# Token numbers laid on 125 partitions by three broadcast loads instead of spread by TensorE

## The reference

```python
w_emb = fake_quant(emb_weight)                 # [125, 128], scale = max|w| / 127
e = w_emb[y]                                   # [8, 512, 128]
x = pad(e, one position in front)
h = relu(depthwise conv of x with 2 taps)      # taps fake-quantized too
h = h + scan(layernorm(h))                     # linear recurrence, 4 heads of 64, normed and mixed
h = h + experts(layernorm(h))                  # 8 experts, 128 -> 512 -> 128, gelu
```

## Time and profile before

| | |
|---|---|
| median of 3 runs | 173.47 us (173.04 to 173.54) |
| the profiled execution | 173.62 us |
| its span, first to last instruction | 171.8 us |
| TensorE busy | 161.1 us, 94% |
| VectorE busy | 131.8 us, 77% |
| ScalarE, Pool busy | 100.1 us, 106.9 us |
| read from memory | 5.15 MB |

### The profile page before, as it was taken

The page is one execution under the profiler, slowest core; times in us unless marked ns, Lnnn a source line. Parts: engine busy times, 40 slices in busy tenths (PEclk is TensorE's granted clock), DMA queues, the critical chain, the costliest instruction groups (busy, mean ns, idle before and its releaser), DMA issues.

```text
span 171.8 us, 3460 instructions
## 1 busy us (share of the span) xinstructions
PE 161.1 (94%) x1149; PEld 137.7 (80%) x1149; DVE 131.8 (77%) x401; ACT 100.1 (58%) x232; POOL 106.9 (62%) x174
## 2 busy tenths in 40 slices
PE   5977999998999999999999999999999999998892
PEld 2666775895765799887668999999999999988791
DVE  3979959735448385997995998989889895668983
ACT  3038999442223532324326867859778597787691
POOL 4437678579995133460403794988969789698600
PEclk9999999999999999999999999999999999999999
DMA  4996000000000000000000000010100101001103
GB/s 147 370 427 257 4 0 2 0 6 0 0 0 0 4 0 0 0 6 0 0 0 0 0 4 0 4 63 0 56 11 0 63 0 65 0 0 67 59 2 122
DMA packets 2181, 7.46 MB, mean 43 GB/s; under 512 B 238, under 2 KB 748, under 8 KB 1908
## 3 DMA queue, kind: packets, MB, share of 16 engines
q1 hardware_dynamic: 2146, 7.23, 10.9%
q10 hardware_dynamic: 18, 0.02, 0.1%
HBM read 5.15 MB, written 2.10 MB: 42 GB/s over the span
## 4 chain that ended last, share of the span: by engine, by line
PE 67%; POOL 13%; issue 7%; ACT 5%; DVE 4%; DMA 2%; POOLq 1%; ACTq 0%; DVEq 0%
PE bank L1305 8%; PE bank L1285 8%; PE bank L1234 7%; PE bank L1149 6%; POOL hid_p L538 6%; PE bank L1143 5%; PE bank L1080 4%; PE bank L1030 4%; PE bank L1086 4%; PE bank L1231 3%; PE bank L1254 3%; POOL rstd L521 3%; PE bank L1111 2%; POOL res L549 2%; PE bank L1055 2%
## 5 line engine op out<-in xcount | busy, mean ns | idle before, releaser
L538 POOL TENSOR_TENSOR hid_p<-hid_f,hid_p 128x256 fp32r<-128x256 f32 x52 | 37.2, 739 | 15.4 <-ACT hid_p L686 13.8
L684 ACT ACTIVATE hid_f<-bank,pa 128x256 f32<-128x256 f32 x64 | 30.7, 487 | 17.5 <-PE bank L1285 14.7
L1285 PE MATMUL bank<-xaT_p,fc_p 128*128 128x256 f32 x192 | 34.8, 293 | 0.2 <-issue 0.2
L1305 PE MATMUL bank<-hid_p,out_hi 128*128 128x256 f32 x128 | 33.0, 293 | 1.7 <-POOL hid_p L538 1.1
L1285 PEld LDWEIGHTS bank<-xaT_p,fc_p 128*128 128x128 f32 x192 | 26.7, 190 | 0.3 <-issue 0.3
L1305 PEld LDWEIGHTS bank<-hid_p,out_hi 128*128 128x128 f32 x128 | 23.3, 188 | 3.6 <-POOL hid_p L538 2.3
L686 ACT ACTIVATE hid_p<-bank,pa 128x256 fp32r<-128x256 f32 x48 | 23.4, 487 | 0.0
L1234 PE MATMUL bank<-pb,xh 128*128 128x128 f32 x128 | 19.5, 275 | 0.0
L521 POOL TENSOR_TENSOR rstd<-spread,neg_half 128x8 f32<-128x8 f32 x8 | 13.2, 1646 | 9.5 <-DVE spread L933 9.5
L1305 PE MATMUL bank<-hid_p,out_lo 128*128 128x256 f32 x64 | 17.8, 279 | 0.0
L1234 PEld LDWEIGHTS bank<-pb,xh 128*128 128x128 f32 x128 | 16.9, 192 | 0.0
(11 more groups left out here) (156 smaller groups left out, 375.0 us busy)
## 6 DMA issues: line engine op xcount, KB each, us to landing
fc_w<-in_fc SPq DMA_DIRECT2D x2, 2048.0 KB, 11.5
out<-res SPq DMA_DIRECT2D x7, 256.0 KB, 2.0
pa<-in_pack_a SPq DMA_DIRECT2D x1, 407.0 KB, 3.2
pb<-in_pack_b SPq DMA_DIRECT2D x1, 384.0 KB, 4.2
out<-res SPq DMA_DIRECT2D x2, 128.0 KB, 1.7
pw<-in_pack_a SPq DMA_DIRECT2D x1, 64.0 KB, 3.2
emb_w<-in_emb SPq DMA_DIRECT2D x1, 62.5 KB
conv_w<-in_conv ACTq DMA_DIRECT2D x1, 1.0 KB
```

What stands on the lines that cost most here:

```text
L538: nc.gpsimd.tensor_tensor(hid_p[1][:, half, c, :], hid_f[:, m % HID_SLOTS, :], hid_p[0][:, half, c, :].bitcast(F32), ALU.subtract).then_in ...
L684: full = nc.scalar.activation(hid_f[:, m % HID_SLOTS, :], src, ACT.Gelu, bias=bias)
L1285: last = mm(fc1_bank(8 * b + n)[:, 0:HALF], fc1_p[w][:, e * HID + c * P:e * HID + (c + 1) * P], xaT_p[m][:, b % 2, half, :], start=(k == 0 ...
L1305: last = mm(out_bank(b, half)[:, half * HALF:(half + 1) * HALF], out_p[w][:, e, c * CH:(c + 1) * CH], hid_p[m][:, half, c, :], start=(c == ...
```

## The change

The integers go straight to 125 partitions. Three loads on ACT's queue read the token numbers of batch 0, of batches 1 to 3 and of batches 4 to 7, each with the partition as its outermost dimension of size 125 and a source that is the same for every partition. `ids_all` takes 16 KB on each of 125 partitions, in the place that `out_hi` takes over later. `one_hot` reads the integers from SBUF and waits for a load at batches 0, 1 and 4. `ids_i`, `ids_b`, `ident_b`, Pool's two casts and one memset, and `spread_ids` with its semaphore are gone; two more products of zeros stand where TensorE spread the first four batches. A tile `spare` keeps the other tiles where they were.

```diff
--- before.py
+++ after.py
+        with ExitStack() as until_gathered:
+
+            ids_all = until_gathered.enter_context(nc.sbuf_tensor("ids_all", [VOC, NB, L], I32))
...
-            ids_i = sb_early("ids_i", [NB, L], I32)
-            ids_b = sb_early("ids_b", [P, L], BF16)
-            ident_b = sb_early("ident_b", [P, P], BF16)
+            spare = sb_early("spare", [P, 832])
...
-        ld_ids, ld_emb, ld_pa, ld_pb = sem("ld_ids"), sem("ld_emb"), sem("ld_pa"), sem("ld_pb")
+        ld_ids = [sem("ld_ids0"), sem("ld_ids1"), sem("ld_ids2")]
+        ld_emb, ld_pa, ld_pb = sem("ld_emb"), sem("ld_pa"), sem("ld_pb")
...
-        def ids_bank(b):
-            return bank[{2: 3, 3: 6}.get(b, b % 2)][0:VOC, :]
...
+        IDS_PARTS = ((0, 1), (1, 4), (4, NB))
...
-                nc.gpsimd.memset(ids_b[:], 0.0).then_inc(pool_const, 1)
-                pool.wait_ge(ident_ready, 2)
-                nc.gpsimd.tensor_copy(ident_b[:], ident).then_inc(ids_ready, 1)
...
-                pool.wait_ge(pool_const, 6)
-                pool.wait_ge(ld_ids, 16)
-                nc.gpsimd.tensor_copy(ids_b[0:NB, :], ids_i[:]).then_inc(ids_ready, 1)
...
                 act.dma_start(conv_w[:], conv).then_inc(ld_conv, 16)
-                act.dma_start(ids_i[:], ids).then_inc(ld_ids, 16)
+                for n, (b0, b1) in enumerate(IDS_PARTS):
+                    act.dma_start(ids_all[:, b0:b1, :], ids[b0:b1].unsqueeze(0).broadcast_to([VOC, b1 - b0, L])
+                                  ).then_inc(ld_ids[n], 16)
...
                 def one_hot(b):
-                    dve.wait_ge(idb_done, b + 1)
+                    for n, (b0, _) in enumerate(IDS_PARTS):
+                        if b == b0:
+                            dve.wait_ge(ld_ids[n], 16)
                     if b >= OH_SLOTS:
                         dve.wait_ge(gat_done, b - OH_SLOTS + 1)
-                    nc.vector.tensor_scalar(onehot[:, b % OH_SLOTS, NCH:EXT * NCH], ids_bank(b), float(VOC - 1),
+                    nc.vector.tensor_scalar(onehot[:, b % OH_SLOTS, NCH:EXT * NCH], ids_all[:, b, :], float(VOC - 1),
                                             number[0:VOC, :], ALU.min, ALU.is_equal).then_inc(oh_ready, 1)
 
-                dve.wait_ge(pool_const, 6)
+                dve.wait_ge(pool_const, 5)
...
-                def spread_ids(b):
-                    if b > 3:
-                        pe.wait_ge(oh_ready, (1, 2, 5, 6)[b - 4])
-                    mm(ids_bank(b), ident_b[:, b:b + 1].broadcast_to([P, VOC]), ids_b[:], start=True,
-                       stop=True).then_inc(idb_done, 1)
-
...
-                pe.wait_ge(pool_const, 6)
+                pe.wait_ge(pool_const, 5)
...
-                pe.wait_ge(ids_ready, 2)
-                spread_ids(0)
-                spread_ids(1)
-                spread_ids(2)
-                pe.wait_ge(amax_all_ready, 1)
-                spread_ids(3)
-                keep_clock(1)
+                keep_clock(3)
...
-                    if 3 < b + 3 < NB:
-                        spread_ids(b + 3)
```

More of the change, by code:

```diff
@@ L207, in build @@
         pool_link, dve_link = sem("pool_link"), sem("dve_link")
-        ids_ready, amax_e_ready, tab_ready = sem("ids_ready"), sem("amax_e_ready"), sem("tab_ready")
+        amax_e_ready, tab_ready = sem("amax_e_ready"), sem("tab_ready")
         attn_g_ready, taps_ready = sem("attn_g_ready"), sem("taps_ready")
         amax_t_done, taps_done = sem("amax_t_done"), sem("taps_done")
-        idb_done, oh_ready, gat_done, h_ready = sem("idb_done"), sem("oh_ready"), sem("gat_done"), sem("h_ready")
+        oh_ready, gat_done, h_ready = sem("oh_ready"), sem("gat_done"), sem("h_ready")
         st1_ready, mv1_ready, rstd1_ready, u_ready = (
```

## The result

The changed kernel takes 199.88 us (median of 4 runs, 199.42 to 200.00) against 173.34 us for the kernel before, run alongside. The ratio is 1.152, 95% interval 1.150 to 1.155. The forecast was 194.0. Its mechanism was given 189 to 199, the whole range was 186 to 200. So the direction is right and the size 6 us short; the measured time lies 0.9 us above the mechanism's own range and 0.1 us inside the wider one.

What follows compares the result with a forecast made beforehand. TensorE, busy 94% of 171.8 us, bounds the kernel, so head delays reach the end in full. 173.6 + 20.1 - 0.5 - 0.5 + 1.5 = 194.2, or 194.0 us against the runs' median; mechanism 189 to 199, range 186 to 200.

Steps and rivals of the forecast that it cites:

- Five engines: New loads at the head: 125 rows are carried by five engines, 25 rows each, 410 KB on each.
- Which load is last, and what it holds up: Head: the third load lands last and delays the fifth one-hot; the second, at 18 to 22 us, costs nothing beyond.
- When it lands: Third load's landing: 31.3 us (30.1 to 33) at 26.6 GB/s per engine; fifth one-hot moves from 11.19, +20.1 us.
- Given back in the rounds: Behind the wait, up to batch 7: two savings of 0.5 us each.
- The first term: Behind the fifth one-hot: statistics of batch 2 follow after about 3.0 us instead of 3.46, -0.5 us.
- The second was nothing: Rounds up to batch 7: shorter one-hots and missing products save 0.5 us (0 to 2.9).
- The slow pace of TensorE: After TensorE's idle time: slower gathers, transposes and powers, 1.2 us a round for none to three rounds, +1.5 us.
- The shorter one-hot: VectorE's one-hot reading SBUF instead of PSUM: 0.45 us taken, bounds 0.29 to 0.75, against 0.75 before.
- The sixteen-engine case: Rival, chance 0.06: the new loads spread over all 16 engines, third landing between 12.6 and 20.3 us; 173.5 to 182.
- Slow reads of a shared stretch: Rival, chance 0.04: reading one stretch of memory 125 times runs at two thirds of the rate; about 202 or more.
- The prologue's 0.4 us: Prologue ahead of the rounds: its own gain of some 0.4 us, expected to drown in the wait.
- ScalarE's queue first: Rival, chance 0.07: the five engines serve ScalarE's queue first, 410 KB land at 17.8 us; about 179.5 to 181.

Runs made afterwards that it cites:

- the run with TensorE busy through the wait: The changed kernel with 20 more products of zeros ahead of the first transposes, where TensorE waited for the third load; 198.82 us.
- The half version: The kernel before, with only batches 4 to 7 laid by one 128-row load behind pack_b, TensorE spreading the first four; 173.95 us, ratio 1.002.
- the run with own stretches: The changed kernel with each of the 125 rows reading its own stretch of the fc1 weights instead of the shared token numbers; 198.93 us.

## Why the prediction was right, and where it was short

The path was right: five engines, the third load, and the wait in front of the fifth one-hot. The landing time was not, and that the measured 199.88 still lies within the stated range is luck: the range went to 200 for the tails of the rivals, while my own sum ended at 199.

**Five engines: right.** The small packets of before told it, 15 more of them appeared, and every run with another row count followed.

**Which load is last, and what it holds up: right.** The third load, then VectorE's fifth one-hot, and behind it TensorE's transposes. The second load came at 27.5, not at 18 to 22, and stayed without cost of its own.

**When it lands: the term that was too small.** Predicted 31.3, measured 37.3, which is the whole error: +20.1 should have been +26.1. The bytes were right. From 20 us on 2.14 MB were still moved, nearly all by the five engines (in the first of these microseconds the others were still ending). These have 3.70 MB in all, so they had done some 1.6 MB by then, 320 KB each in the 17.7 us from 2.3 on: an estimated 18 GB/s. At the 26.6 that I took from the earlier trace rows it would have been 12.0 us; the missing 5.7 us are nearly all of the error. I took the rate of engines whose rows are all dealt alike; beside rows dealt otherwise all 16 together ran at 241 to 283 GB/s over 3 to 15 us. My upper end of 33 was no bound for this: it left contention out.

**Given back in the rounds: 0.5 + 0.5 predicted, 0.7 measured**, from the run with TensorE busy through the wait. The first term, the statistics of batch 2 that need not wait, was 1.0: they come 2.5 us behind the one-hot (37.30 to 39.78), not 3.46. The second was nothing: 0.3 was lost again, by the difference, for which no run gives a cause. The half version shows some 0.2 won in steady rounds.

**The slow pace of TensorE: 1.5 predicted, 1.1 measured.** It was over by the gather at 44.69.

**The shorter one-hot: 0.45 taken, 0.48 measured**, against 0.75 from PSUM.

**The rivals.** ScalarE's queue was not served first. The sixteen-engine case was put at 173 to 182; made real by 128 rows it is 177.6, and in line of need 173.75. Slow reads of a shared stretch had the right size (about 202) for the wrong reason, as the run with own stretches shows. The prologue's 0.4 us were not won in any run: the first one-hot waited for its load in every one that had it come that way. Two sums have small slips that bear on nothing: ScalarE's queue first gives 179.1 by its own terms (173.5 + 6.6 - 1.0), not 179.5, and the forecast 194.1.

## What to carry to other kernels

Ask of each load how its rows are dealt before asking how many bytes it has: give it 128 rows even where 125 are used (200 us became 177.6), and do not cut it into pieces of other row counts (187 to 193 us here). Then put the loads on one queue in the order in which they are needed (177.6 became 173.75, with order and queue changed together). And before taking work off an engine in a loop of four engines, find which one sets the pace: here the products and one-hots that went had been hidden.

## What was not expected of the hardware

Loads of other row counts slow the 128-row loads beside them: over 3 to 15 us the engines, all busy, moved 272 (125 rows), 241 (120 + 5), 262 (112 + 13) and 266 GB/s (64 + 64), against 400 before and 376 and 382 with 128. A 16 KB row of another load took 775 to 981 ns in place of 611, and in the 125-row case this held on engines that carried none of these rows. Five engines with nobody beside them kept 26.8 GB/s each.

The profile's granted clock is no sure sign of TensorE's pace. In the run with 120 + 5 rows it shows 0.50 from 27 to 30 us, which is 1.2 of 2.4 GHz, and the gather at 27.87 took 1.91 us; the changed kernel's gather behind its wait took the same 1.91 us under 1.00.
